# Eight transformer tiles a batch, one core: the order of the first tile's work against the constants and weight parts

## The reference

```
x = every second row of each segment of 256            # 8 x 3 tiles of 128 rows, 256 wide
h = softmax(x x^T / 16) x                              # per tile
n = layernorm(h)
bound = circ_conv(n, bind_key); holo_t = sum_s d^(t-s) bound_s   # over the 384 rows of a batch, d = sigmoid(decay)
h = h + n + gate * circ_corr(holo, unbind_key)
h = h + ffn(layernorm(h))
```

## Time and profile before

| | us |
|---|---|
| median of 3 runs | 790.74 |
| the runs | 790.24, 790.74, 827.2 |
| profiled execution, its own time | 790.91 |
| its span, first to last instruction | 789.1 |
| mean granted TensorE clock in it | 0.974 |

### The profile page before, as it was taken

The page is one execution under the profiler, slowest core; times in us unless marked ns, Lnnn a source line. Parts: engine busy times, 40 slices in busy tenths (PEclk is TensorE's granted clock), DMA queues, the critical chain, the costliest instruction groups (busy, mean ns, idle before and its releaser), DMA issues.

```text
span 789.1 us, 14516 instructions
## 1 busy us (share of the span) xinstructions
PE 740.8 (94%) x4736; PEld 645.8 (82%) x4736; DVE 652.3 (83%) x1516; ACT 525.7 (67%) x1308; POOL 290.2 (37%) x393
## 2 busy tenths in 40 slices
PE   4878999999999999999999999999999999999995
PEld 3657888888888888888888888888888888888884
DVE  3655888888888989889889889888888898898864
ACT  4455577567667676686675685776676766766654
POOL 1334423343343252353344334333432532533321
PEclk9578999999999999999999999999999999999999
DMA  8300000000000000000000000000000000000000
GB/s 332 108 14 7 2 1 21 1 21 21 1 21 21 2 21 5 16 22 1 21 21 2 21 22 0 22 21 1 22 21 1 8 8 1 9 1 7 8 1 21
DMA packets 11611, 17.28 MB, mean 22 GB/s; under 512 B 1232, under 2 KB 10504, under 8 KB 11024
## 3 DMA queue, kind: packets, MB, share of 16 engines
q1 hardware_dynamic: 11536, 16.35, 6.1%
HBM read 13.20 MB, written 3.15 MB: 21 GB/s over the span
## 4 chain that ended last, share of the span: by engine, by line
PE 42%; ACT 24%; DVE 22%; issue 9%; POOL 1%; DMA 1%; SPq 0%; POOLq 0%; ACTq 0%; DVEq 0%
PE ctl L474 10%; PE ctl L490 8%; PE ctl L451 5%; ACT L813 4%; ACT L923 4%; ACT L824 3%; ACT ge L846 3%; DVE hm_hi L1087 3%; PE pb L451 3%; PE ctl L493 3%; ACT work L816 2%; ACT work L820 2%; DVE tied L1258 2%; DVE both L1284 2%; DVE gl L1101 2%
## 5 line engine op out<-in xcount | busy, mean ns | idle before, releaser
L366 POOL TENSOR_TENSOR hm_lo<-gl,mexp 128x256 fp32r<-128x256 f32 x144 | 111.3, 799 | 335.2 <-DVE gl L1101 335.2
L474 PE MATMUL ctl<-w2e_hi,hm_hi 128*128 128x512 f32 (+1 forms) x432 | 161.0, 382 | 9.5 <-DVE hm_hi L1087 9.2
L474 PE MATMUL ctl<-w2e_lo,hm_hi 128*128 128x512 f32 (+1 forms) x432 | 149.9, 361 | 0.0
L864 ACT ACTIVATE work<-ctl 128x256 f32<-128x256 f32 (+1 forms) x144 | 70.7, 491 | 91.1 <-PE ctl L493 91.1
L474 PEld LDWEIGHTS ctl<-w2e_hi,hm_hi 128*128 128x128 f32 x432 | 82.4, 191 | 27.0 <-DVE hm_hi L1087 15.5
L490 PE MATMUL ctl<-w2e_hi,hm_lo 128*128 128x512 f32 (+1 forms) x432 | 102.0, 362 | 0.1
L1087 DVE TENSOR_TENSOR hm_hi<-ge,mexp 128x256 fp32r<-128x256 f32 x144 | 79.3, 577 | 22.1 <-ACT ge L846 15.8
L474 PEld LDWEIGHTS ctl<-w2e_lo,hm_hi 128*128 128x128 f32 x432 | 82.6, 191 | 11.2
L451 PEld LDWEIGHTS pa<-x1T,par 128*128 128x128 f32 x768 | 89.4, 192 | 1.1
L451 PE MATMUL pa<-x1T,par 128*128 128x128 f32 x768 | 89.6, 275 | 0.0
L490 PEld LDWEIGHTS ctl<-w2e_hi,hm_lo 128*128 128x128 f32 x432 | 74.5, 188 | 14.7 <-POOL hm_lo L366 0.8
(11 more groups left out here) (174 smaller groups left out, 1741.9 us busy)
## 6 DMA issues: line engine op xcount, KB each, us to landing
work<-params_dram SPq DMA_DIRECT2D x3, 1152.0 KB, 10.1
xT<-turned_dram SPq DMA_DIRECT2D x24, 128.0 KB, 2.3
out_dram<-y SPq DMA_DIRECT2D x24, 128.0 KB, 1.7
xa<-x_dram SPq DMA_DIRECT2D x16, 128.0 KB, 2.3
par<-params_dram SPq DMA_DIRECT2D x1, 1280.0 KB, 12.7
work<-params_dram SPq DMA_DIRECT2D x2, 512.0 KB, 11.0
xa<-x_dram SPq DMA_DIRECT2D x8, 119.0 KB
par<-params_dram SPq DMA_DIRECT2D x1, 512.0 KB, 15.7
```

The source lines that it names most:

```text
L366: TT(hm[1][:, j, c, :], gl[:, c, :], pairs(tile, j, c), ALU.mult).then_inc(done, 1)
L474: mm(dst[:, a:z], hm[0][:, j, c, :], w2e[i][:, c, a:z], start=(c == 0 and i == 0), stop=False)
L864: AF(tan[tile.s][:, 1:kinds, j, :], ctl_t[:, D:kinds * D].rearrange("p (a d) -> p a d", a=kinds - 1), ACT.Tanh, scale=0.5)
```

## The change

In PE's program the binding product moves behind the attention product of tile 0 (half 0) and behind the transposes of xn of tile 0 (half 1). In DVE's program `rates()` moves behind the reduction of tile 1 and is cut in two: the second half, `branch_rates()`, follows xf of tile 0. `gated_mix()` moves behind the scan. Of w2b's low parts, k = 0 is made behind xf, ahead of the reduction of tile 2; the low part of w2e and parts k = 1, 2 are made behind the router's choice and `shared_lo` of tile 0, and count set_dve once more, so that PE and ACT wait for set_dve 3 ahead of the first round. No instruction is added or taken away, apart from the one more semaphore count. ACT's, POOL's and SP's programs stay as they are (but for the count that ACT waits for).

```diff
--- before.py
+++ after.py
@@ -562,7 +562,7 @@
 
                     if t.low == 0:
                         pe.wait_ge(par_in[3], 16)
-                        pe.wait_ge(set_dve, 2)
+                        pe.wait_ge(set_dve, 3)
                         pe.wait_ge(set_act, 4)
                     passed(pe, sl1_v, t)
                     if m.exists():
@@ -579,8 +579,6 @@
                     if t.exists():
                         passed(pe, me_sb, t, per=2, step=1)
                     nc.tensor.transpose(pc[:, 0:P], ex[:, :], ident).then_inc(eT_ps, 1)
-                    if f.low == 0:
-                        bound_and_back(1)
 
                 if t.exists():
                     passed(pe, hm1_v, t, per=3, step=1)
@@ -598,6 +596,8 @@
                         passed(pe, smax_v, f.at(1))
                     pe.wait_ge(x_in[f.x], 16 * (f.turn + 1))
                     mm(pd[:, 0:D], eT[:, :], xa[f.x][:, :], start=True, stop=True).then_inc(att_ps, 1)
+                    if f.low == 0:
+                        bound_and_back(0)
 
                 if n.exists() and t.exists():
                     passed(pe, x1_v, n)
@@ -627,6 +627,8 @@
                     for q in range(KD):
                         last = nc.tensor.transpose(pc[:, q * P:(q + 1) * P], xn[:, q * P:(q + 1) * P], ident)
                     last.then_inc(xnT_ps, 1)
+                    if f.low == 0:
+                        bound_and_back(1)
 
                 if n.exists() and t.exists():
                     passed(pe, x1T_sb, n)
@@ -651,8 +653,6 @@
                     hidden(pa, P, w1e, range(EC), x1T, 2 * KD, e2_ps)
 
                 if z.exists():
-                    if z.low == 1:
-                        bound_and_back(0)
                     pe.wait_ge(xT_in[z.s], 16 * (z.b + 1))
                     if f.exists():
                         passed(pe, mv2_v, f)
@@ -889,7 +889,7 @@
                     AF(tw[:, :], dif[:, :], ACT.Tanh, scale=0.5).then_inc(tw_sb, 1)
                     if t.low == 0:
 
-                        act.wait_ge(set_dve, 2)
+                        act.wait_ge(set_dve, 3)
                     if t.low == 2:
 
                         act.wait_ge(set_pool, 4)
@@ -1042,6 +1042,9 @@
                 link(V.tensor_scalar(dcol, dcol, 1.0, None, ALU.add))
                 link(V.reciprocal(dcol, dcol))
                 link(V.tensor_scalar(decays[:, :], decays[:, :], dcol, None, ALU.mult))
+
+            def branch_rates():
+
                 link(V.tensor_scalar(swc, swc, 1.0, None, ALU.add))
                 link(V.reciprocal(swc, swc))
                 link(V.tensor_scalar(omsw, swc, -1.0, 1.0, ALU.mult, ALU.add))
@@ -1064,8 +1067,9 @@
                 dve.wait_ge(set_act, 2)
                 w2bm = staged("w2b").rearrange("p (k m) -> p k m", k=3)
                 for k in ks:
-                    V.scalar_tensor_tensor(w2b[:, k, :], w2b[:, k, :].bitcast(fp32), part[k], w2bm[:, k, :],
-                                           ALU.mult, ALU.add)
+                    last = V.scalar_tensor_tensor(w2b[:, k, :], w2b[:, k, :].bitcast(fp32), part[k], w2bm[:, k, :],
+                                                  ALU.mult, ALU.add)
+                return last
 
             def routed_weight_low():
 
@@ -1181,8 +1185,6 @@
                     passed(dve, xnT_ps, f, back=1)
                     V.tensor_scalar(xn[:, :], h[:, :], mv1[:, 0:1], rs1[:, :], ALU.subtract,
                                     ALU.mult).then_inc(xn_v, 1)
-                    if f.low == 0:
-                        gated_mix()
 
                 if m.exists() and not last_in:
                     gates(m)
@@ -1196,6 +1198,8 @@
                         last = V.tensor_tensor_scan(holo[f.s][:, q, :], decays[:, :], pc[:, q * P:(q + 1) * P], carry,
                                                     ALU.mult, ALU.add)
                     last.then_inc(scan_v, 1)
+                    if f.low == 0:
+                        gated_mix()
 
                 if m.exists() and not last_in:
                     velocity_gates(m)
@@ -1204,8 +1208,6 @@
                     output(o)
 
                 if f.exists():
-                    if f.low == 0:
-                        shared_weight_low(range(2))
                     passed(dve, retr_ps, f)
                     passed(dve, hx_g, f)
                     passed(dve, base_g, f, back=1)
@@ -1222,6 +1224,9 @@
                     passed(dve, mv2_v, f)
                     V.tensor_scalar(xf[f.s][:, :], h2[:, :], mv2[:, 0:1], rs2[:, :], ALU.subtract,
                                     ALU.mult).then_inc(xf_v, 1)
+                    if f.low == 0:
+                        branch_rates()
+                        shared_weight_low(range(1))
 
                 if m.exists() and not last_in and not t.newest():
                     products(m)
@@ -1231,11 +1236,8 @@
                     passed(dve, ex_sb, z, back=1)
                     V.tensor_scalar(sc[:, :], pd[:, 0:P], -float(D) ** -0.5, None, ALU.mult, ALU.min,
                                     accum_out=nmx[:, z.s:z.s + 1]).then_inc(smax_v, 1)
-                    if z.low == 0:
+                    if z.low == 1:
                         rates()
-                    if f.exists() and f.low == 0:
-                        shared_weight_low(range(2, 3))
-                        routed_weight_low()
 
                 if n.exists():
                     last_ps, last_g, back = (u1_ps, hl1_g, -1) if t.exists() else (u2_ps, hl2_g, 1)
@@ -1274,6 +1276,9 @@
                     V.scalar_tensor_tensor(side[:, :], lg[:, :], -2.0, side[:, :], ALU.mult, ALU.mult,
                                            accum_out=dif[:, :]).then_inc(dif_v, 1)
                     shared_lo(f, s1_sb, sh1, sab1, sl1_v)
+                    if f.low == 0:
+                        routed_weight_low()
+                        shared_weight_low(range(1, 3)).then_inc(set_dve, 1)
 
                 if m.exists():
                     if last_in:
```

## The result

| | before | changed |
|---|---|---|
| median | 790.24 us (20 runs) | 788.0 us (20 runs) |
| lowest to highest | 787.39 to 827.2 | 786.98 to 789.95 |
| profiled execution, own time | 790.91 | 788.04 |
| its span | 789.1 | 786.3 |
| router product of tile 0 on PE | 24.64 | 22.31 |

The ratio to the kernel before is 0.9978, with a 95% interval of 0.9970 to 0.9986: faster by 1.1 to 2.4 us, 1.7 in the middle, and within 2%. One run of the kernel before, 827.2, was a slow execution and isn't in the ratio. The forecast was 789.8 with a gain of 0.9 from 790.74, and a range of 788.0 to 792.0. The direction held; the gain was about twice what I had.

What follows compares the result with a forecast made beforehand. PE, busy 94%, bounds the kernel from about 66 us, so only the front can gain. Of 5.7 us of earlier attention, 1.9, 1.9 and 1.0 are spent, leaving 0.9: 789.8 from 790.74, range 788.0 to 792.0.

Steps and rivals of the forecast that it cites:

- What bounds: Whole kernel: PE's pace from about 66 us; the change gains only what brings slot 0's first round forward.
- Step 1: Tile 0's attention product, no longer behind the key matrices: ends at 9.04 instead of 14.79, 5.7 us forward.
- Step 2: Binding product fills the next chain; late mix sets the retrieval at 15.03 instead of 18.88, 3.8 us forward.
- Step 3: Tile 0's router product waits for DVE's reduction of tile 2: 22.7 instead of 24.64, 1.9 us left.
- Step 4: DVE's tail of 4.34 us ahead of the first round: shared control at 32.65 instead of 33.57, 0.9 us left.
- Rival D: DVE's tail held up or longer than its room; at 5.83 us it is 0.6 slower, 791.4; chance 0.1.
- The sum: First shared control product 0.9 us earlier, everything behind it moving with it: 789.8 against the median 790.74.
- Rival B: PE's clock already up at tile 0's retrieval, which takes 1.13: 0.9 more gain, 788.9; chance 0.2.
- Rival C: PE's new hole ahead of the shared control keeps the clock low longer: 0.6 slower, 791.3; chance 0.2.

Runs made afterwards that it cites:

- second experiment: Changed kernel with part k = 0 of w2b moved behind the mix and the branch rates into DVE's tail, nothing ahead of tile 2's reduction: 788.29 us, ratio 0.9979.
- third experiment: Changed kernel with w2e's low part behind tile 2's reduction, w2b parts k = 0, 1 behind the mix, branch rates and k = 2 in the tail: 785.12 us.
- first experiment: Changed kernel with the low part of w2e made behind the reduction of tile 2 instead of in DVE's tail: 785.6 us, ratio 0.9949 to the kernel before.

## Why the prediction was right, and where it was off

**What bounds.** Right: the steady part kept its shares, and the change worked only by moving slot 0.

**Step 1** (attention at 7.98 to 9.04): 7.73 to 8.95. Right; the small parameters landed 0.1 sooner. That it hangs on the move of DVE's `rates()` as well as on PE's order is what the experiment with PE's order alone shows.

**Step 2** (mix at 14.25, retrieval at 15.03): 14.13 and 14.93. Right.

**Step 3** (router product at 22.7, released by the reduction): 22.31. Right in kind; part k = 0 took 1.02, so it lay at the lower bound, and the 1.53 of the branch rates were right (19.41 to 20.94). The second experiment shows what stood there: without that work the router product is released by xfT.

**Step 4** (tail 4.34, shared control at 32.65): DVE's tail was 27.83 to 32.25, 4.42, the shared control 32.35; PE had been idle for 2.15 where I had 1.6 to 2, since the clock was up when it got there. The low part of w2e took 2.56 with POOL idle and 3.07, 2.87 and 2.98 with POOL at work (before, first and third experiment); I had 2.42 for it. In all three it ended 2.4 behind the end of the POOL sum that was running when it started. This agrees with the exclusive port pair of the Trainium skill (SBUF — State Buffer, "SBUF: two separate sides"); in the third experiment POOL's next sum, `base`, was the one to be held up, 3.04 instead of 0.72. Rival D had no part in it. (Its own sum was a little high: a tail of 5.83 from 28.2 gives 34.08, 0.5 slower and not 0.6.) What the step left out is that the low part had an idle place before, between the reduction and the router's choice; the first experiment puts 2.6 us on that.

**The sum.** This is the term that failed in size: "0.9 us". At the shared control the gain was 1.2 in the profiled pair, 0.3 more than forecast, by step 3. Behind it I had written that everything "moves with it". It didn't move alike: the attention product of tile 1 came at 35.72 instead of 37.36 (1.6 sooner), the retrieval of tile 1 at 41.47 instead of 43.62 (2.15 sooner), and the span ended 2.8 sooner. From the shared control to the attention product it took 3.37 instead of 3.79, since two products ran at the full clock; behind it the next rise came at 36.2 instead of 38.9. The retrieval of tile 4, where the clock is full in all profiles, shows what was left; the kernel before first, then the changed kernel in its three profiled executions:

```profile
130.93 1.13 PE L646 MATMUL cd<-mix,holo 128*128 128x256 f32 x4
...
128.38 1.13 PE L648 MATMUL cd<-mix,holo 128*128 128x256 f32 x4
...
128.59 1.13 PE L648 MATMUL cd<-mix,holo 128*128 128x256 f32 x4
...
128.24 1.13 PE L648 MATMUL cd<-mix,holo 128*128 128x256 f32 x4
```

That is a gain of 2.3 to 2.7 in all three. At the shared control it was 1.2, 2.7 and 1.3. The 2.7 are of the execution in which the second half of the binding product took 1.38 (1.91 in the others) and the retrieval 1.13 (2.08): 1.5 of them are the clock, and 1.2 are left. So in these profiles the order gives 1.2 to 1.3 us at the shared control, and the other 1.2 to 1.4 at tile 4 arise behind it, where the profiles run the same program and differ in where the clock was low. The kernel before has one profile here, so how much of that second part belongs to the change and how much to chance stays open; the ratio over all runs, 1.1 to 2.4 us, holds both.

**Rival B** (clock up at the retrieval, 788.9) was what one of three profiled executions of the changed kernel did. Its time, 788.21, was no better than the 788.04 of the first one: the lead of 1.4 us was down to 0.3 by the retrieval of tile 1. **Rival C** (the hole keeps the clock low, 791.3) fell as a forecast: with the hole the clock rose for the first round's large products at 35.9, 36.2 and 36.8 in the three executions, 3.6 to 5.9 behind the hole's end, where the profile of before has 38.9, 8.7 behind. In two of the three it was already up within the hole. But in those two it fell again right behind the hole, at 32.8 and 32.6, and was low until the rise at 36.2 and 35.9, while in the first experiment, which has no hole there, it was up without a break from 26.5 to 40.6. So a price of the hole in clock is neither shown nor excluded, and part of what the first and third experiments gain may be that.

## What to carry to other kernels

Where several engines hand a latency chain to each other, ask of each piece of set-up work not "how long is it" but "which gate stands behind it and how long does its engine stand idle elsewhere": the same 2.6 us of DVE held up the first round in the tail and left no wait on PE some 6 us sooner, in a gap in which the kernel before had had them all along. Two moves can also need each other: the reorder on PE brought 1.0 us alone, that on DVE cost 2.0 alone, and together they brought 2.7. Taking work off one gate pays only if it doesn't land ahead of the next (second experiment); moved into the idle stretches it brought 3 us beyond the changed kernel's own gain of some 2. And compare differences between two rows of one profile: they agreed to 0.01 us between executions whose absolute instants differed by 1.4.

## What the runs showed of the hardware

The granted clock of the front differs between executions of one program: at 29.5 to 32.5 it was 1.00 in one and 0.50 in the other. The spans differed by 0.1, so a change of a microsecond can't be read from the clock of one profile.

So does the clock at the end, where PE is busy about half of the time. The changed kernel's profiles on the first and the second chip had the retrieval near 706 us within 0.1 (706.28 and 706.18), but the spans are 786.4 and 788.0:

```profile
770.00:786.00 16.00, 8.01 (x49) 6.81 (x47) 6.17 (x10) 6.00 (x13) 2.56 (x2) 0.89 0.05 17
...
770.00:788.00 18.00, 9.76 (x48) 8.52 (x47) 6.09 (x10) 5.91 (x13) 2.56 (x2) 0.69 0.05 15
```

The second had the lower clock in its last stretch, 0.69 where the first had 0.89, and ended 1.6 later, more than what the change is worth at the shared control.

The clock column reads 1.00 ahead of the first recorded change, whatever the engine does: in the changed kernel the retrieval took 2.08 (the low level) in a stretch where the column has 1.00. There the durations of known products tell the level, 1.13 or 2.08 for this one.
